# First LSTM sweep of a graph network layer: input projection of two steps at a time, and the gate bias moved from matmuls to the copies and the activations

## The reference, cut to what matters

```python
x_proj = einsum('btd,gd->btg', x, W_ih) + b_ih + b_hh      # 1024 gate columns
gates = xp + h @ W_hh.T
i, f, g, o = split(gates, 4)
c = sigmoid(f) * c + sigmoid(i) * tanh(g)
h = sigmoid(o) * tanh(c)
```

## Time and profile before

| | |
|---|---|
| median of 3 runs | 2604.55 us (2603.65 to 2613.02) |
| profiled execution, its own time | 2609.78 us |
| its span | 2607.9 us |
| TensorE busy | 2304.9 us (88%) |
| VectorE busy | 1761.6 us (68%) |
| ScalarE busy | 1521.7 us (58%) |
| GpSimd busy | 118.7 us (5%) |

### The profile page before, as it was taken

How to read it: one execution, slowest core, us unless ns; L and a number is a source line. 1 busy time by engine, 2 the same in 40 slices (tenths; PEclk the granted TensorE clock), 3 DMA queues, 4 the chain that set the end, 5 groups by cost and what they waited for, 6 DMA issues and landing times.

```text
span 2607.9 us, 46559 instructions
## 1 busy us (share of the span) xinstructions
PE 2304.9 (88%) x14839; PEld 1974.3 (76%) x14839; DVE 1761.6 (68%) x4053; ACT 1521.7 (58%) x2861; POOL 118.7 (5%) x121
## 2 busy tenths in 40 slices
PE   4578989999999999999898999998887887888844
PEld 3467868888888888888786888888887887888623
DVE  5755887777777777777477455556665665566688
ACT  2354448888888888888533444445554555555315
POOL 4232000000000000000000000000000000000000
PEclk9889999999999999999999999999999999999975
DMA  3222320000000000000331122123332332333103
GB/s 96 70 70 79 97 74 25 27 26 24 27 25 28 23 28 26 29 23 21 108 95 44 63 86 86 79 89 116 110 115 82 110 117 87 106 114 110 39 8 90
DMA packets 95188, 174.13 MB, mean 67 GB/s; under 512 B 8983, under 2 KB 69411, under 8 KB 94769
## 3 DMA queue, kind: packets, MB, share of 16 engines
q1 hardware_dynamic: 63378, 86.63, 10.1%
q10 hardware_dynamic: 28108, 81.19, 9.9%
q0 software_dynamic: 3584, 4.76, 0.6%
HBM read 114.14 MB, written 58.36 MB: 66 GB/s over the span
## 4 chain that ended last, share of the span: by engine, by line
PE 62%; DVE 14%; issue 8%; ACT 5%; ACTq 2%; DVEq 1%; POOL 0%; DMA 0%; POOLq 0%
PE psum L608 22%; PE psum L603 11%; PE psum L758 9%; PE psum L718 8%; DVE scr L1535 3%; DVE scr L1533 2%; ACT scr L1018 2%; PE psum L726 2%; PE psum L660 2%; PE psum L670 2%; PE psum L714 2%; DVE scr L1357 2%; DVE scr L1531 1%; DVE bufB L1537 1%; ACTq L1029 1%
## 5 line engine op out<-in xcount | busy, mean ns | idle before, releaser
L931 ACT ACTIVATE counts<-psum 125x500 fp32r<-125x500 f32 (+1 forms) x663 | 720.1, 1121 | 160.9 <-PE psum L603 159.1
L608 PE MATMUL psum<-halves,counts 125*125 125x512 f32 x2500 | 743.9, 418 | 2.8 <-ACT counts L931 2.0
L1383 DVE TENSOR_TENSOR wx<-rs_buf 128x500 bf16<-128x500 bf16 (+2 forms) x1326 | 641.9, 531 | 132.0 <-PE psum L603 72.2
L758 PE MATMUL psum<-bufB,wx 128*128 x4800 | 603.9, 283 | 90.6 <-DVE bufB L1537 81.6
L758 PEld LDWEIGHTS psum<-bufB,wx 128*128 128x128 f32 x4800 | 565.3, 194 | 129.0 <-issue 118.1
L608 PEld LDWEIGHTS psum<-halves,counts 125*125 125x125 f32 x2500 | 418.6, 187 | 59.9 <-issue 4.8
L603 PE MATMUL psum<-wx 128*125 128x250 bf16 x2550 | 399.3, 277 | 5.5 <-DVE wx L1383 5.3
L603 PEld LDWEIGHTS psum<-wx 128*125 128x125 bf16 x2550 | 320.9, 139 | 91.0 <-DVE wx L1383 8.6
L718 PE MATMUL psum<-bufA,wx 128*128 (+1 forms) x1600 | 232.7, 289 | 0.0
L718 PEld LDWEIGHTS psum<-bufA,wx 128*128 128x128 f32 x1600 | 194.9, 192 | 23.6 <-issue 0.2
L1018 ACT ACTIVATE scr<-scr 128x125 f32<-128x125 f32 x300 | 92.2, 307 | 168.6 <-DVE scr L1535 168.6
(11 more groups left out here) (257 smaller groups left out, 2464.8 us busy)
## 6 DMA issues: line engine op xcount, KB each, us to landing
bufA<-gates_of_x ACTq DMA_DIRECT2D x144, 500.0 KB, 3.4
gates_of_x<-bufB SPq DMA_DIRECT2D x48, 500.0 KB, 2.6
sums_by_feature<-scr SPq DMA_DIRECT2D x51, 125.0 KB, 2.0
x_times_eps_plus_sums<-rs_buf ACTq DMA_DIRECT2D x10, 625.0 KB
wx<-in_x_dram SPq DMA_DIRECT2D x25, 250.0 KB
x_plus_mix<-wx SPq DMA_DIRECT2D x25, 250.0 KB, 4.8
scr<-x_times_eps_plus_sums SPq DMA_DIRECT2D x50, 125.0 KB
x_times_eps_plus_sums<-scr SPq DMA_DIRECT2D x50, 125.0 KB
```

The lines of the kernel that those rows point to most:

```text
L608: return mm(psum[0:TP, 3 + v, :], cnt[v][:, hi, :], xhl[:, hi, :, :].rearrange("p s d -> p (s d)"), start=(hi == 0), stop=(hi == NT - 1))
L758: return mm(half_gates(u, m, slot[0])[:, slot[1], :], whhv[:, k, (2 * gate + m) * P:(2 * gate + m + 1) * P], h, start=False, stop=(k == 1) ...
L931: fn(cnt[v][:, :, 2 * GW * u:2 * GW * u + GW * g].rearrange("p h c -> p c h"), psum[0:TP, u % 3, 0:g * KEYS].rearrange("p (c h) -> p c h", ...
L1383: last = tt(to[:, 0:gs, :, :], tab2[:, 0:k, :].unsqueeze(1).broadcast_to([P, gs, k, 2]), keysT[v][:, part_, g0:g0 + gs, :].unsqueeze(2).br ...
```

## The change

- The projection is made for a pair of steps at once: `project(p, v, g)` issues, for one gate, four f32 matmuls of 250 columns (two strips of 125, steps 2p and 2p+1). The PSUM of a gate now holds both steps: two blocks of 250, each with 125 for either step. There is no bias matmul; `bias24` and `sel24` are gone.
- In `pair`, gates i and g of the next pair are projected between the recurrences of the pair's two steps, f and o behind the second one.
- Each of VectorE's copies takes one block m of both steps (250 columns) and adds the bias, a column of 128 values (`bias_c`); there are eight for a pair, placed between the operations of the two steps. The copies of the first pair are split by step (`keep_first`).
- ScalarE adds the bias in the activation, which takes a separate instruction for each block: 8 of 125 columns a step where there were 4 of 250. Sigmoid of i comes first, then tanh of g, with a semaphore of its own (`tg_act`).
- SP stores a pair in one DMA (24 instead of 48). The loops of all engines turn over two pairs (12 turns); the last pair, which projects nothing, stands behind the loop.
- The bias: two DMAs of 1024 single elements on GpSimd's queue and one addition on VectorE. The splitting, SP's five copies, the selector's memset and GpSimd's affine_select go.

```diff
-        pre_out = [bufB[:, 256 + v * 4 * HC:256 + (v + 1) * 4 * HC].rearrange("p (g n) -> p g n", g=4) for v in range(2)]
+        pre_out = [bufB[:, 256 + v * 8 * HC:256 + (v + 1) * 8 * HC].rearrange("p (s g c j) -> p s g c j", s=2, g=4, c=2) for v in range(2)]
...
+        bias_c, bias_2 = sb("bias_c", 8), sb("bias_2", 8)
-        GATE_ORDER = (2, 0, 1, 3)
+        GATE_ORDER = (0, 2, 1, 3)
...
-            with sp.Fori(1, LS // 2) as i:
-                for v in range(2):
-                    sp.wait_ge(S["kept_v"], 8 * i + 4 * v + 4)
-                    sp.dma_start(pre_d[ds(2 * i + v, 1), :, :].rearrange("t p n -> (t p) n"),
-                                 pre_out[v].rearrange("p g n -> p (g n)")).then_inc(S[f"pre_st{v}"], 16)
+            with sp.Fori(0, LS // 4) as i:
+                for v in (1, 0):
+                    sp.wait_ge(S["kept_v"], 16 * i + (24 - 8 * v))
+                    sp.dma_start(pre_d[ds(4 * i + (4 - 2 * v), 2), :, :].rearrange("t p n -> p t n"),
+                                 pre_out[v].rearrange("p s g c j -> p s (g c j)")).then_inc(S[f"pre_st{v}"], 16)
...
-            for m in range(8):
-                for k, name in enumerate(("L0_ffn_b_ih", "L0_ffn_b_hh")):
-                    pool.dma_start(bias_f[m:m + 1, k, :], a[name][m * P:(m + 1) * P].rearrange("(a n) -> a n", a=1)).then_inc(S["ld_bias"], 16)
+            with nc.allow_non_contiguous_dma(reason="two vectors of 1024 elements, onto the partitions"):
+                for c, name in ((bias_c, "L0_ffn_b_ih"), (bias_2, "L0_ffn_b_hh")):
+                    pool.dma_start(c[:, :], a[name].rearrange("(m p) -> p m", p=P)).then_inc(S["ld_bias"], 16)
...
-            def project(t, u):
-                for g in GATE_ORDER:
-                    mm(psum[:, 4 * u + g, 0:HC], bias24[:, :], sel24[:, g * HC:(g + 1) * HC],
-                       start=True, stop=False, skip_group_check=True)
-                    for m in (2 * g, 2 * g + 1):
-                        for c in range(2):
-                            last = mm(gate_bank(u, m), wihv[:, c, m * P:(m + 1) * P],
-                                      ls_in[:, ds(t, 1), c, :].rearrange("p t j -> p (t j)"),
-                                      start=False, stop=False, skip_group_check=True)
-                    last.then_inc(S["pre_mm"], 1)
-            def recur(weights, h, u, gates, done):
-                for m in gates:
-                    for c in range(2):
-                        last = mm(gate_bank(u, m), weights[c][:, m * P:(m + 1) * P], h[c],
-                                  start=False, stop=(c == 1), skip_group_check=True)
+            def project(p, v, g):
+                for c0 in range(2):
+                    m = 2 * g + c0
+                    for k in range(2):
+                        last = mm(psum[:, 4 * v + g, c0 * HC:(c0 + 1) * HC].rearrange("p (s j) -> p s j", s=2),
+                                  wihv[:, k, m * P:(m + 1) * P], ls_in[:, ds(2 * p, 2), k, :],
+                                  start=(k == 0), stop=False, skip_group_check=True)
+                last.then_inc(S["pre_mm"], 1)
+            def recur(v, s, g, done):
+                for c0 in range(2):
+                    m = 2 * g + c0
+                    for k in range(2):
+                        last = mm(psum[:, 4 * v + g, c0 * HC + s * CH:c0 * HC + (s + 1) * CH], whb[k][:, m * P:(m + 1) * P],
+                                  h_low[:, s, k, :], start=False, stop=(k == 1), skip_group_check=True)
                 last.then_inc(done, 1)
-            def first_step(t, u):
-                h = [h_low[:, u, c, :] for c in range(2)]
-                pe.wait_ge(S["h_v"], 1 + t)
-                pe.wait_ge(S["kept_v"], 4 * t + 1)
-                recur(whb, h, u, (4, 5), S["g_mm"])
-                pe.wait_ge(S["kept_v"], 4 * t + 2)
-                recur(whb, h, u, (0, 1), S["i_mm"])
-                pe.wait_ge(S["kept_v"], 4 * t + 3)
-                recur(whb, h, u, (2, 3), S["f_mm"])
-                pe.wait_ge(S["kept_v"], 4 * t + 4)
-                recur(whb, h, u, (6, 7), S["o_mm"])
-                pe.wait_ge(S["so_act"], 1 + t)
+            def first_step(p, v, s):
+                pe.wait_ge(S["h_v"], 2 * p + (s + 1))
+                for n_, (g, done) in enumerate(zip(GATE_ORDER, ("i_mm", "g_mm", "f_mm", "o_mm"))):
+                    pe.wait_ge(S["kept_v"], 8 * p + (2 * n_ + 2))
+                    recur(v, s, g, S[done])
+            def pair(p, v):
+                first_step(p, v, 0)
+                pe.wait_ge(S["so_act"], 2 * p + 1)
+                for g in GATE_ORDER[0:2]:
+                    project(p + 1, 1 - v, g)
+                first_step(p, v, 1)
+                for g in GATE_ORDER[2:4]:
+                    project(p + 1, 1 - v, g)
             pe.wait_ge(S["w_low"], 2)
-            project(0, 0)
-            with pe.Fori(0, LS // 2 - 1) as i:
-                for u in range(2):
-                    first_step(2 * i + u, u)
-                    project(2 * i + u + 1, 1 - u)
-            first_step(LS - 2, 0)
-            project(LS - 1, 1)
-            first_step(LS - 1, 1)
+            for g in GATE_ORDER:
+                project(0, 0, g)
+            with pe.Fori(0, LS // 4) as i:
+                for v in range(2):
+                    pair(2 * i + v, v)
+            for s in range(2):
+                first_step(LS // 2 - 1, 0, s)
+            pe.wait_ge(S["so_act"], LS + 1)
...
-            def time_step(now, u):
+            act.wait_ge(S["bias_v"], 1)
+            def gate_act(to, v, s, g, function, done):
+                for c in range(2):
+                    last = fn(to[:, c * CH:(c + 1) * CH], psum[:, 4 * v + g, c * HC + s * CH:c * HC + (s + 1) * CH], function,
+                              bias=bias_c[:, 2 * g + c:2 * g + c + 1])
+                last.then_inc(done, 1)
+            def time_step(now, v, s):
+                act.wait_ge(S["i_mm"], now)
+                gate_act(s_if[:, 0, :], v, s, 0, ACT.Sigmoid, S["si_act"])
                 act.wait_ge(S["g_mm"], now)
-                fn(tg_c[u][:, 0, :], psum[:, 4 * u + 2, 0:HC], ACT.Tanh)
-                act.wait_ge(S["i_mm"], now)
-                fn(s_if[:, 0, :], psum[:, 4 * u, 0:HC], ACT.Sigmoid).then_inc(S["si_act"], 1)
+                gate_act(tg_c[s][:, 0, :], v, s, 2, ACT.Tanh, S["tg_act"])
                 act.wait_ge(S["f_mm"], now)
-                fn(s_if[:, 1, :], psum[:, 4 * u + 1, 0:HC], ACT.Sigmoid).then_inc(S["sf_act"], 1)
+                gate_act(s_if[:, 1, :], v, s, 1, ACT.Sigmoid, S["sf_act"])
                 act.wait_ge(S["o_mm"], now)
-                fn(s_o[:, :], psum[:, 4 * u + 3, 0:HC], ACT.Sigmoid).then_inc(S["so_act"], 1)
+                gate_act(s_o, v, s, 3, ACT.Sigmoid, S["so_act"])
                 act.wait_ge(S["c_v"], now)
-                fn(th[:, :], tg_c[1 - u][:, 1, :], ACT.Tanh).then_inc(S["th_act"], 1)
-            with act.Fori(0, LS // 2) as i:
-                for u in range(2):
-                    time_step(act.snap(2 * i + u + 1), u)
+                fn(th[:, :], tg_c[1 - s][:, 1, :], ACT.Tanh).then_inc(S["th_act"], 1)
+            with act.Fori(0, LS // 4) as i:
+                for v in range(2):
+                    for s in range(2):
+                        time_step(act.snap(4 * i + (2 * v + s + 1)), v, s)
+            for s in range(2):
+                time_step(LS - 1 + s, 0, s)
...
-            def bias_parts():
-                dve.wait_ge(S["ld_bias"], 256)
-                tt(bias_f[:, 2, :], bias_f[:, 0, :], bias_f[:, 1, :], ALU.add).then_inc(S["bias_v"], 1)
...
+            def biases():
+                dve.wait_ge(S["ld_bias"], 32)
+                tt(bias_c[:, :], bias_c[:, :], bias_2[:, :], ALU.add).then_inc(S["bias_v"], 1)
...
-            def time_step(now, u, h, gate_o, tanh_c):
+            dve.wait_ge(S["bias_v"], 1)
+            def keep(p, v, m):
+                g, c = m // 2, m % 2
+                dve.wait_ge(S["pre_mm"], 4 * p + (GATE_ORDER.index(g) + 1))
+                ts(pre_out[v][:, :, g, c, :], psum[:, 4 * v + g, c * HC:(c + 1) * HC].rearrange("p (s j) -> p s j", s=2),
+                   bias_c[:, m:m + 1], None, ALU.add).then_inc(S["kept_v"], 1)
+            def keep_first(m):
+                g, c = m // 2, m % 2
+                dve.wait_ge(S["pre_mm"], GATE_ORDER.index(g) + 1)
+                for s in range(2):
+                    last = ts(pre_kept[s][g // 2][:, g % 2, c * CH:(c + 1) * CH], psum[:, g, c * HC + s * CH:c * HC + (s + 1) * CH],
+                              bias_c[:, m:m + 1], None, ALU.add)
+                last.then_inc(S["kept_v"], 1)
+            def enter(now, s):
                 dve.wait_ge(S["si_act"], now)
-                tt(prod[:, 0, :], s_if[:, 0, :], tg_c[u][:, 0, :], ALU.mult)
+                dve.wait_ge(S["tg_act"], now)
+                tt(prod[:, 0, :], s_if[:, 0, :], tg_c[s][:, 0, :], ALU.mult)
+            def cell(now, s):
```

(71 more changed lines are left out.)

24 lines of the change are left out of this document (3 added, 21 removed).

## The result

The changed kernel is slower: 2766.3 us median of 4 runs (2766.0 to 2774.4) against 2605.3 for the kernel before (median of 4), a ratio of 1.062 [1.059, 1.065]. The forecast was 2534.5 (2515 to 2562) and 0.93 for faster; the measured time lies 204 us above the range, at the 2767 that the prediction gave its rival 4 with a chance of 0.03.

A forecast was written before the change was run, and what follows sets the result against it. TensorE's own work was taken to bound the bf16 sweep; the sweep 70.5 us shorter, 1 saved in bias preparation and 1.5 lost to its loads made 70 off 2604.55: 2534.5 us, range 2515 to 2562.

The forecast's parts named there:

- rival 4: Later f32 sweeps: bias added behind the sum changes h's rounding, a fourth sweep costs 233 us, about 2767; chance 0.03.
- a count of fetches other than 144: Later sweeps: gate fetches differing from 144 (three sweeps) were named as a sign that the prediction was wrong.
- A pair: bf16 sweep: two steps take 9.2 us against 12.17, with two gates of wide projection at 3.4.
- The stall at the last copies: TensorE before the o recurrence: waits 0.26 us for VectorE's last two copies, 0.35 a pair with its restart.
- The chain: A step's path through ScalarE and VectorE: stays hidden in halves of 4.8 and 4.4 us, the second with 0.2 slack.
- rival 1: bf16 sweep: each half of a pair waits for h, pair 10.2 to 11.6 us, 2558 to 2591; chance 0.12.
- Table loads: ScalarE in the bf16 sweep: at most one load per loop turn, 12 or 13 in all, costing about nothing.
- rival 2: bf16 sweep: a table load shows in the chain, 13 to 16 us, 2548 to 2550; chance 0.06.
- The first projection: Head of the bf16 sweep: 32 passes below full speed, 6.8 plus 1.7 lost, 8.5 us.
- The stores: Pair stores, 24 of 1 MB: land in 5.2 us and cost nothing below 11 us a store.
- The front: Before the sweep: bias preparation saves 1 us, its loads delay the second block of x by 1.5 us.
- Rival 3: Projection: 250-column passes cost 2 x 0.136 us, so no change beyond 13 us; chance 0.03.

The follow-up runs named there:

- e1: The changed kernel with the start flag off for a gate's second block, so one start a bank: 2534.2 us, ratio 0.972.
- e2: The changed kernel with the bound for ending the sweeps eight times as wide, 2^-13 for 2^-16: 2769.8 us, 192 fetches.
- e4: The kernel before with half the bound for ending the sweeps, 2^-17 for 2^-16: 2604.7 us, 144 fetches.
- e1b: The kernel of e1 run again, on the same chip as e9: 2534.9 us, ratio 0.972.
- e8: The kernel before with the bias moved into copies and activations, no bias matmuls, steps not paired, tanh of g still first: 2595.1 us, ratio 0.994.
- e9: e1 with one block of the next pair's projection issued ahead of the o recurrence in a pair's first step: 2525.8 us, ratio 0.968.
- e7: e1 with the old gate order, tanh of g ahead of sigmoid of i: 2540.3 us, ratio 0.974.
- e6: The kernel of e1 with the bound for ending the sweeps at 2^-2: 2065.0 us, 48 fetches, one sweep.
- e5: The changed kernel with the bound for ending the sweeps at 2^-2: 2296.7 us, 96 fetches, two sweeps.

## Why the prediction was wrong

**The step that failed** is one that has no number in the sum: the later sweeps were carried over at three, and there were four, +235 us. The sum costed what the change does to the time of its own stage, and took what the stage hands on as unchanged. Rival 4 did name a fourth sweep, and its price was right (233 us, 2767), but its mechanism was rounding, argued down to 0.03 and refuted by e1, e2 and e4; that the measured time is its 2767 is a right price with a wrong cause. The prediction had also named a count of fetches other than 144 as a sign that it was wrong, and this sign came. The mechanism that decided was in the diff: start=(k == 0) inside a loop over two blocks of one bank, where the kernel before had one bias matmul with a start over all 250 columns and nothing but start=False behind it. Each of those 200 matmuls was costed at 0.21 us; that it was also the one start of its bank was not asked. With the flag mended (e1) the time is 2534.2, against 2534.5 forecast. That they agree to 0.3 us is in part luck: the forecast was 70 us below a median of 2604.55, and e1 and e1b lie 73 and 75 below the kernel before as it ran beside them (2607.6 and 2610.3).

**The terms**, measured in the changed kernel:

- A pair: 9.14 us (9.2). Two gates of wide passes, 1544.21 to 1547.66, take 3.45 (3.4). Right in sum, but not in its parts: the prediction gave 42 us to the bias matmuls and 49 to the width. By e8 a gate of 125 columns without its bias matmul takes 0.905 (3.62 / 4), against 1.29 with it and 1.73 for a wide one. So some 77 us went with the 200 bias matmuls, and the width itself is worth 2 x 0.905 - 1.73, 0.08 a gate or 8 us.
- The stall at the last copies: 0.28 idle (0.26), with its restart 0.4 by e9 (0.35). Right; a copy with an add is 0.47 to 0.48 long.
- The chain: small activations 2.15 / 8, about 0.26 apart (0.26). The halves are 4.80 and 4.34 (4.8 and 4.4), h 0.69 and 0.20 ahead of its need (0.7 and 0.2), no wait for h. Right, so rival 1 did not come about.
- Table loads: 12 in the sweep (12 or 13). The load at 1542.22 put the first activation 0.65 behind its recurrence instead of 0.43, hidden. Load to activation is 1.29 again, without the drain of about 1.38 us that the Trainium skill ("ScalarE: Activation LUTs", What ACT_TABLE_LOAD costs) puts on top. Had the second load stayed, e7 shows 8 us of rival 2's 13 to 16.
- The first projection: 6.85 us from 1426.00 to the first recurrence at 1432.85, where the prediction had 8.5. In e1 the same 32 passes take 8.5 (1427.37 to 1435.90). The two rows:

```profile
1426.00 7.01 PE L699 MATMUL psum<-bufA,wx 128*128 128x250 f32 x32 [3.07 <-POOL rs_buf L461]
```

```profile
1427.37 8.69 PE L699 MATMUL psum<-bufA,wx 128*128 128x250 f32 x32 [3.12 <-POOL rs_buf L461]
```

  The granted clock from 1430 to 1435 us was 1.00 in the changed kernel and 0.79 in e1 (0.81 in the kernel before); e6 and e7 show 6.85 too, e1b, e2, e5 and e9 8.5. So what is lost there is clock, 8.5 holds for five of these eight profiles, and the profile of the changed kernel had the luck of the full one. This is 1.7 of the 3 us by which its sweep beat the forecast (-73.5 for -70.5). e1's sweep of 238.2 (-72.0) beat it by 1.5, which is what 24 pairs of 9.14 instead of 9.2 give.
- The stores: landing after 3.9 (5.2), nothing waits for them. Right.
- The front: the second block of x at 24.95 for 24.31, 0.6 later (1.5). The bias preparation is one operation of 0.58. What either is worth at the end lies below the scatter of 5 us or so in when the sweep starts, so it stays unmeasured.
- Rival 3 falls with the 9.14 us.

What stays open: how much e8 lost to the waits and how much to the clock is an estimate from its rows and windows, and which units of the state were poor was not measured.

## What to carry to other kernels

When a change removes a matmul, ask what else it did besides its arithmetic: a start=True belongs to its PSUM bank, and whoever takes over must give it once for the bank, not once for each group in it. Where a loop repeats until something agrees, its count is a term of the sum: ask of every edit ahead of it whether it changes what the loop starts from, and look at a count (here the fetches) before any duration. An operation moved off the bound engine is worth its time only if what replaces it finds a gap on the engine that takes it: the bias edit took 78 us of work off TensorE, but alone it gave 12 us; in the pairs the copies that took the bias over were hidden but for 0.28 us a pair.
